# A two-layer graph network kernel: the opening chunks of x taken by rows, later ones by halves, and several steps in other places of the engines' orders

## What is computed

```python
def _ada_gcn(xn, weight, bias):                  # xn = x transposed: (N=512, B=64, L=128)
    x_norm = xn / jnp.maximum(jnp.linalg.norm(xn, axis=-1, keepdims=True), 1e-12)
    mean_sim = jnp.einsum('nbl,mbl->nm', x_norm, x_norm) / B
    k = max(int(N * 0.3), 1)
    ...                                          # keep the k most similar others of each node
    A = jnp.where(mask, mean_sim, 0)
    deg = A.sum(axis=0)
    dinv = jnp.where(deg > 0, jax.lax.rsqrt(deg), 0)
    An = dinv[:, None] * A * dinv[None, :]
    xw = jnp.einsum('nbl,lo->nbo', xn, weight)
    return jnp.einsum('sd,sbl->dbl', An, xw) + bias

x = _layernorm(x + L0(x, adj, bias))
x = _layernorm(x + L1(x, adj, W_lang, W_grav, W_V, W_O, gate_logit, log_sigma))
```

## Time and profile before

| | us |
|---|---|
| median of 3 runs | 957.14 (956.38 to 957.51) |
| the profiled execution | 958.09 |
| its span, first to last instruction | 956.4 |
| PE busy | 915.4 (96% of the span) |
| DVE busy | 750.3 (78%) |
| ACT busy | 535.0 (56%) |
| POOL busy | 306.9 (32%) |

### The profile page before, as it was taken

The page is one execution under the profiler, slowest core; times in us unless marked ns, Lnnn a source line. Parts: engine busy times, 40 slices in busy tenths (PEclk is TensorE's granted clock), DMA queues, the critical chain, the costliest instruction groups (busy, mean ns, idle before and its releaser), DMA issues.

```text
span 956.4 us, 18776 instructions
## 1 busy us (share of the span) xinstructions
PE 915.4 (96%) x6800; PEld 537.2 (56%) x6800; DVE 750.3 (78%) x1696; ACT 535.0 (56%) x956; POOL 306.9 (32%) x390
## 2 busy tenths in 40 slices
PE   3999999989999999999999999999999999999993
PEld 3777796555555555556464646555555555555451
DVE  5787398768888888888787888888887878786766
ACT  6787656675646455555546464646373646463531
POOL 3777372235040404040505050505050504041410
PEclk9999999999999999999999999999999999999997
DMA  6454230110413232313141413232222323121211
GB/s 266 176 200 155 87 90 1 45 45 6 96 57 88 64 81 66 89 53 104 38 119 29 116 33 109 42 101 48 94 55 87 58 84 71 73 57 45 56 46 44
DMA packets 101704, 75.84 MB, mean 79 GB/s; under 512 B 80544, under 2 KB 80672, under 8 KB 99616
## 3 DMA queue, kind: packets, MB, share of 16 engines
q1 hardware_dynamic: 101664, 75.32, 27.1%
HBM read 38.86 MB, written 16.78 MB: 58 GB/s over the span
## 4 chain that ended last, share of the span: by engine, by line
issue 50%; PE 19%; POOL 13%; DVE 11%; ACT 4%; DMA 1%; POOLq 1%; DVEq 0%; ACTq 0%
POOL arena L438 6%; PE bank L530 2%; PE bank L264 2%; PE bank L266 2%; PE bank L265 2%; POOL arena L443 2%; PE bank L537 2%; PE bank L536 2%; POOL arena L477 2%; ACT arena L1149 1%; POOL rn_parts L460 1%; POOL part_rest L458 1%; DVE stats L1636 1%; PE bank L500 1%; PE pair L264 1%
## 5 line engine op out<-in xcount | busy, mean ns | idle before, releaser
L264 PE MATMUL bank<-arena 128*128 128x512 f16 (+2 forms) x1056 | 293.8, 302 | 6.1 <-DVE arena L1690 2.0
L266 PE MATMUL bank<-arena 128*128 128x512 f16 (+2 forms) x1056 | 293.3, 301 | 0.0
L265 PE MATMUL bank<-arena 128*128 128x512 f16 (+2 forms) x1056 | 293.3, 301 | 0.0
L264 PE MATMUL pair<-arena 128*128 128x512 f16 (+1 forms) x400 | 151.2, 378 | 0.0
L265 PE MATMUL pair<-arena 128*128 128x512 f16 (+1 forms) x400 | 150.9, 378 | 0.0
L266 PE MATMUL pair<-arena 128*128 128x512 f16 (+1 forms) x400 | 150.8, 378 | 0.0
L264 PEld LDWEIGHTS bank<-arena 128*128 128x128 f16 x1056 | 103.6, 98 | 67.4 <-DVE arena L1690 4.3
L266 PEld LDWEIGHTS bank<-arena 128*128 128x128 f16 x1056 | 103.8, 98 | 63.5 <-issue 0.8
L265 PEld LDWEIGHTS bank<-arena 128*128 128x128 f16 x1056 | 103.8, 98 | 54.7 <-issue 0.3
L460 POOL TENSOR_TENSOR sq_parts<-cf,zero 128x4 bf16<-128x4 f32 x16 | 3.4, 210 | 397.2 <-DVE cf L1739 397.2
L438 POOL TENSOR_TENSOR arena<-arena 128x512 f32<-128x512 f32 x64 | 81.1, 1268 | 60.0 <-ACT arena L1059 59.6
(11 more groups left out here) (337 smaller groups left out, 1930.0 us busy)
## 6 DMA issues: line engine op xcount, KB each, us to landing
arena<-in_x SPq DMA_DIRECT2D x33, 1024.0 KB, 5.5
out_dram<-arena SPq DMA_DIRECT2D x15, 1024.0 KB, 4.3
arena<-arena SPq DMA_TRANSPOSE x75, 3.2
arena<-in_w_grav_t SPq DMA_DIRECT2D x1, 1024.0 KB, 7.4
arena<-in_w_lang_t SPq DMA_DIRECT2D x1, 1024.0 KB, 5.2
arena<-in_w_v SPq DMA_DIRECT2D x1, 1024.0 KB, 8.0
arena<-in_w_o_t SPq DMA_DIRECT2D x1, 1024.0 KB, 9.2
out_dram<-arena SPq DMA_DIRECT2D x4, 256.0 KB, 2.4
```

The source lines that it names most:

```text
L264: pe.matmul(dst, ah, bh, start=start, stop=False)
L265: pe.matmul(dst, ah, bl, start=False, stop=False)
L266: return pe.matmul(dst, al, bh, start=False, stop=stop)
```

## The change

It moves instructions and splits some. Of new work there are 29 small products on PE whose result nobody reads (`keep_warm`, into a bank that is cleared later), and three more waits per chunk in PE's loop. The parts:

1. Chunk 0 is loaded in two halves, and squared in one half and two rows. DVE adds its rows as they come.
2. ACT loads the table that has the root before its first instruction, and not ahead of the first root.
3. Chunks 0 and 1 are normalised and made high row by row; later chunks by halves. POOL makes low parts row by row for all chunks, and PE waits for each row.
4. `spread(c + 1)` stands ahead of the rows of chunk c, and no longer `spread(c + 2)`; `item_sums(c + 2)` in their middle, and no longer `item_sums(c + 3)`. ACT has a new order: second half of `high(c - 1)`, the squares of chunk c + 2, first half of `high(c)`, `root(c + 1)`.
5. `keep_warm(16)` before PE's first product, `keep_warm(9)` behind the first `item_sums`, `keep_warm(4)` behind the second.
6. POOL makes `mask` behind chunk 1 and not ahead of chunk 0.
7. The squares of W_V and adj stand behind ACT's copies of the turned blocks, in another buffer, and not ahead of `cross_out(0)`. `deviation(0)` stands ahead of the root of `magn`.
8. PE transposes `magn` behind chunk 2 of the second pass, and spreads the root behind chunk 4, not 1. DVE's maximum stands behind its first count, and `scales` behind its second.
9. On ACT `cross_out(2)` and `cross_out(3)` stand ahead of the high part of the first group's x.

PE at the program's start: before, the sums and spreads of three chunks stand ahead of the first row of products (L515 is the first product of a row).

The diff, cut to its core:

```diff
+            for half in range(2):
+                mine = slice(half * CL // 2, (half + 1) * CL // 2)
+                sp.dma_start(xc[0][:, mine, :], x_chunk[0][:, mine, :]).then_inc(s["first_half"] if half == 0 else x_loaded[0], 16)
-            for c in range(SLOTS):
+            for c in range(1, SLOTS):
                 sp.dma_start(xc[c], x_chunk[c]).then_inc(x_loaded[c], 16)
...
+            def keep_warm(n):
+                for i in range(n):
+                    pe.matmul(bank[4][:, 0:P], ones[:], ident[:], start=True, stop=True)
+
+            keep_warm(16)
...
+            def rows_01(c, slot, t, first=False, last=False):
+
+                pe.wait_ge(s["xn_l_ready"], c * CL + (t + 1))
+                gram(c, (0, 1), first=first, last=last, ts=range(t, t + 1))
 
             item_sums(0, 0)
+            keep_warm(9)
             spread(0, 0)
             item_sums(1, 1)
+            keep_warm(4)
+            rows_01(0, 0, 0, first=True)
+            rows_01(0, 0, 1)
             spread(1, 1)
             item_sums(2, 0)
-            rows_01(0, 0, first=True)
+            rows_01(0, 0, 2)
+            rows_01(0, 0, 3)
+            rows_01(1, 1, 0)
+            spread(2, 0)
+            rows_01(1, 1, 1)
+            item_sums(3, 1)
+            rows_01(1, 1, 2)
+            rows_01(1, 1, 3)
             with pe.Fori(0, (NC - 4) // 2) as j:
-                for t in (1, 2):
-                    rows_01(j * 2 + t, t % 2)
+                for u in (2, 3):
+                    c = j * 2 + u
+                    spread(c + 1, (u + 1) % 2)
+                    rows_01(c, u % 2, 0)
+                    rows_01(c, u % 2, 1)
+                    item_sums(c + 2, u % 2)
+                    rows_01(c, u % 2, 2)
+                    rows_01(c, u % 2, 3)
...
-                if c == 1:
+                if c == 2:
+                    pe.wait_ge(s["magn_ready"], 5)
+                    pe.wait_ge(s["magn_x"], 1)
+                    pe.transpose(bank[4][0:8, 0:P], magn[:], ident[:]).then_inc(s["magn_all_ready"], 1)
+                if c == 4:
 
                     pe.wait_ge(s["magn_root"], 2)
...
+            act.preload_act_table_set("sqrt_and_others")
...
+            def high(c, ts):
+
+                n = 1 if c < 2 else len(ts)
...
+            square(0, 0)
+            square(0, 1)
+            square(1, 0)
             root(0)
+            square(1, 1)
             repeat(0)
-            square(2)
-            for c in range(NC):
+            square(2, 0)
+            high(0, range(0, CL // 2))
+            square(2, 1)
+            root(1)
+            for c in range(1, NC):
+                repeat(c)
+                high(c - 1, range(CL // 2, CL))
+                if c + 2 < NC:
+                    square(c + 2, 0)
+                    square(c + 2, 1)
+                high(c, range(0, CL // 2))
                 if c + 1 < NC:
                     root(c + 1)
...
-            for n, i in enumerate((1, 0, 2, 3)):
+            for n, i in enumerate((1, 0, 3)):
...
+            act.wait_ge(s["w_in2"], 16)
+            act.activation(squares2, w_raw[2], ACT.Square, accum_out=magn[:, 2:3]).then_inc(s["magn_ready"], 1)
...
+            deviation(0)
             act.wait_ge(s["scale_steps"], 2)
...
+            cross_out(2)
+            cross_out(3)
             act.wait_ge(s["w_scaled"], 3)
             act.wait_ge(s["w_l_ready"], 2)
             act.activation(first_x_h, first_x, ACT.Copy).then_inc(s["x_h_ready"], GB)
 
-            cross_out(2)
-            cross_out(3)
...
             def normalise(c):
                 dve.wait_ge(s["spread_ps"], c + 1)
+                n = 1 if c < 2 else CL // 2
...
+                    between(i)
...
+            def scales(step):
+                if step == 0:
+                    dve.wait_ge(s["magn_all_ready"], 1)
...
+                if step != 1:
+                    return
```

More of the change, by code:

```diff
@@ L392, in _ @@
             pool.tensor_copy(ident_b[:], ident[:]).then_inc(s["picks_made"], 1)
[L393 to L407 removed]
+            for c in range(NC):
+                if c == 2:
+                    pool.wait_ge(s["small_in"], 64)
+                    pool.affine_select(out=mask[:], in_=adj_sb[:], compare_op=ALU.not_equal, fill=0.0, base=0,
+                                       pattern=[[-1, P]], channel_multiplier=1).then_inc(s["consts_made"], 1)
+                for t in range(CL):
+                    pool.wait_ge(s["xn_h_ready"], c * CL + t + 1)
+                    pool.tensor_tensor(xn_l[:, c * CL + t, :], xc[c % SLOTS][:, t, :], xn_h[:, c * CL + t, :],
+                                       ALU.subtract).then_inc(s["xn_l_ready"], 1)
             def low(dst, raw, hi, pieces, done):
@@ L551, in turn @@
                 return pe.transpose(dst, S[:, i, j * P:(j + 1) * P], ident[:])
-            def rows_01(c, slot, first=False, last=False):
-                if not isinstance(c, int) or c + 2 < NC:
-                    spread(c + 2, slot)
-                if first:
-                    for t in range(CL // 2):
-                        pe.wait_ge(s["first_low"], t + 1)
-                        gram(c, (0, 1), first=True, ts=range(t, t + 1))
-                else:
-                    pe.wait_ge(s["xn_l_ready"], c + 1)
-                    gram(c, (0, 1), ts=range(0, CL // 2))
-                if not isinstance(c, int) or c + 3 < NC:
-                    item_sums(c + 3, 1 - slot)
-                if first:
-                    pe.wait_ge(s["xn_l_ready"], 1)
-                gram(c, (0, 1), last=last, ts=range(CL // 2, CL))
+            def rows_01(c, slot, t, first=False, last=False):
+                pe.wait_ge(s["xn_l_ready"], c * CL + (t + 1))
+                gram(c, (0, 1), first=first, last=last, ts=range(t, t + 1))
@@ L582, in _ @@
+            for c in range(NC - 2, NC):
+                if c + 1 < NC:
+                    spread(c + 1, (c + 1) % 2)
+                for t in range(CL):
+                    rows_01(c, c % 2, t, last=(c == NC - 1))
             finish_diagonal(0)
@@ L943, in repeat @@
                                ACT.Copy).then_inc(s["rinv_ready"], 1)
-            def high(c):
-                act.wait_ge(s["xn_ready"], c + 1)
-                act.activation(xn_h[:, c * CL:(c + 1) * CL, :], xc[c % SLOTS], ACT.Copy).then_inc(s["xn_h_ready"], 1)
-            square(0)
-            square(1)
+            def high(c, ts):
+                n = 1 if c < 2 else len(ts)
+                for t in range(ts[0], ts[-1] + 1, n):
+                    act.wait_ge(s["xn_ready"], c * CL + t + n)
+                    act.activation(xn_h[:, c * CL + t:c * CL + t + n, :], xc[c % SLOTS][:, t:t + n, :],
+                                   ACT.Copy).then_inc(s["xn_h_ready"], n)
+            square(0, 0)
+            square(0, 1)
+            square(1, 0)
             root(0)
+            square(1, 1)
             repeat(0)
-            square(2)
-            for c in range(NC):
+            square(2, 0)
[9 more added lines that the diff above has]
+                high(c, range(0, CL // 2))
                 if c + 1 < NC:
                     root(c + 1)
-                    repeat(c + 1)
-                high(c)
-                if c + 3 < NC:
-                    square(c + 3)
+            high(NC - 1, range(CL // 2, CL))
             def s_out(dst, src):
@@ L978, in _ @@
                 act.activation(squares, w_raw[i], ACT.Square, accum_out=magn[:, i:i + 1]).then_inc(s["magn_ready"], 1)
-            act.wait_ge(s["magn_ready"], 4)
-            act.activation(squares[:, 0, 0:P], adj_sb[:], ACT.Square,
-                           accum_out=magn[:, 4:5]).then_inc(s["magn_ready"], 1)
             cross_out(0)
             cross_out(1)
-            act.wait_ge(s["magn_ready"], 5)
-            act.wait_ge(s["xn_l_ready"], NC)
+            act.wait_ge(s["magn_ready"], 3)
+            act.wait_ge(s["xn_l_ready"], NC * CL)
             act.wait_ge(s["gram_full"], 2)
@@ L1352, in _, with pick @@
             C, U = T + COUNTS, T + 2 * COUNTS
-            def pick(pair, n, between=lambda: None):
+            def pick(pair, n, between=lambda step: None):
                 r0 = 2 * pair
@@ L1394, in pick @@
                 n += 2
-                between()
                 for i in range(COUNTS):
```

86 lines of the change are left out of this document (46 added, 40 removed).

## The result

| | before | after |
|---|---|---|
| median of the runs | 957.71 us (20 runs, 956.24 to 959.95) | 953.67 us (20 runs, 951.43 to 956.53) |
| ratio | | 0.9956 [0.9948, 0.9964] |
| profiled execution, its span | 958.09, 956.4 us | 956.53, 954.8 us |

The change makes the kernel 4 us faster. The forecast was 5.2 us. The execution that was profiled here was the slowest of the 20, so the kernel after was profiled once more (experiment e12): 953.40 us, span 951.7.

A forecast was written before the change was run, and what follows sets the result against it. PE was taken to bound the kernel, idle mainly at the opening. The terms, -6.7 at the first pass's end and +1.5 in the second pass, make -5.2: 957.14 - 5.2 = 951.9 us, range 948.6 to 955.4.

The forecast's parts named there:

- The opening: Chunk 0 to the first pass's rows: first row of products at 15.7 against 23.7, rows done 8.4 us earlier on PE.
- Rival (c): First pass: the ring becomes the bound, PE waits at each spread, 0.6 us a chunk gives 959.1; chance 0.09.
- the ring: Each chunk's spread, normalise, high and low within one 5.38 us period; forecast to fit and priced at nothing.
- Rival (d): Opening: the warm-up does not raise the pace and delays the sums; 3.5 us lost, 955.4; chance 0.08.
- rival (a): PE's pace falls in a new idle time, at 12 to 15 or 101 to 104; costs 1.7 us, 953.6; chance 0.15.
- The end of the first pass: ACT, not PE, sets `cross_out(0)`: at 102.4, 6.7 us earlier, so 6.7 of PE's 8.4 us arrive.
- The second pass: Scales 3.8 us later, PE waits 1.2 at the turn and again before `first_project(0)`; PE 1.5 us late at the degrees.
- POOL's low part of x: Second pass: takes 6.07 us, ends at 146.6 in old times, and delays PE's `first_project(0)` by 0.8 us more.
- idle times of 1.2 us in the second part that cost nothing speak against: Argument against the pace falling in a new idle time: idle times of 1.2 us in the second part cost nothing.
- the stretch of the earlier trace: PE at granted clock 0.50 at 196 to 199, behind 2 us idle, costing up to 1.7 us; kept in the sum.

The follow-up runs named there:

- e12: The kernel after once more, unchanged, profiled again; 953.05 us, ratio 0.9956.
- e4: The kernel after without the three `keep_warm` calls of the opening; 954.92 us, ratio 0.9968.
- e7: The kernel after with 12 filler products and with part 9 alone undone; 955.46 us, ratio 0.9977.
- e1: The kernel after with parts 7 to 9 undone, so parts 1 to 6 alone; 956.86 us, ratio 0.9993.
- e9: Parts 1 to 6 and 9, filler products, e6's moved block product, squares of W_V and W_O on VectorE behind GpSimd's last low part; 949.50 us.
- e3: The kernel after plus 12 filler products nobody reads, 7 ahead of the first diagonal and 5 ahead of the turns; 953.79 us, ratio 0.9954.
- e6: e3 with a block column of the first group's upper product moved ahead of the turns of h for items 2 and 3; 951.48 us.
- e8: Parts 1 to 6 alone (e1) with the same 12 filler products as e3; 954.17 us, ratio 0.9970.
- e11: e10 with e6's moved block product in the first group; 953.79 us, ratio 0.9965.
- e10: Parts 1 to 6 and 9 with filler products (16 and 5), without parts 7 and 8; 954.97 us, ratio 0.9975.
- e5: e3 with the squares of two weights on VectorE in its idle time at 95.6 us and the scales at their old place; 956.33 us.
- e2: Parts 7 to 9 alone, on the kernel before; 958.50 us, ratio 1.0005.

## Why the prediction was right, and where it was not

**The opening: right.** `ssum(0)` was ready at 8.64 (forecast: 7.7). The second half of chunk 0 landed only at 6.5, which cost 0.9, and `keep_warm(16)` hid most of it, as it ended at 9.2 anyway. With the forecast in brackets, the sums started at 9.23 (8.9), the spread at 12.18 (11.9; but the terms that the prediction lists there, 9.8 + 0.7 + 1.05 + 0.63, make 12.2), the first row at 16.18 (15.7), and the spreads of chunks 3 and 4 at 27.83 and 33.27 (27.65, 33.05). From there a chunk took 5.38 us. Rival (c), the ring, did not occur. DVE and ACT grew by 0.13 and 0.12 us a chunk, under the 0.15 and 0.2 I had put on them, and POOL to 4.83 and not 4.51. Rival (d) is refuted by the rows at 16.46 and e4, and the fall of rival (a) in the opening did not occur in either profile of after; e7 shows that it can.

**The end of the first pass: right.** ACT and not PE sets it: `cross_out(0)` at 102.65 and 102.55 (102.4), 6.5 us earlier and not 8.4. e1 with one square more has 104.77, e9 with one less 101.01.

**The second pass: the mechanism right, one term too small.** With the clock held (e3) the scales' turn to wait came as written: ACT's high part of W_V at 114.55 (121.4 - 6.7 = 114.7), first group's x at 130.01 (129.4), the wait at the turn 1.08 us (1.2), the degrees at 160.73 (161.2). One step was wrong without harm: POOL's low part of x took 5.17 us and not 6.07, and PE did not wait for it; instead it waited 1.01 at the third diagonal, as ACT was still scaling x. The sum of the losses, 1.2 us, was forecast as 1.5.

What failed is the step "idle times of 1.2 us in the second part that cost nothing speak against" rival (a), and its price of 1.7 us. In the profiled execution of after the low stretch lasted from 104.3 to 111.1, not 3.5 us. From the first `turn` to the wait at the third diagonal PE needed 135.43 - 105.27 = 30.2 us, and 27.4 in e12 (105.16 to 132.56): **2.8 us for one fall of the clock**. The rival gave it a chance of 0.15 as something that happens or not; it happens in part of the executions. The 20 times of after go with the mean granted clock: five from 951.4 to 951.9 have 0.994, two of 956.5 have 0.987 and 0.989, and the rest lie between. Behind which gap each of them lost is not shown, but the profiles with 0.994 (e6, e8, e11) show no fall between 0 and 930 us.

**Two agreements are luck.** The five fast times lie at the forecast of 951.9, but the forecast had kept the stretch of the earlier trace rows in its sum. If they had no fall at all, what they saved there, 1.5 us in e12, made up for what the groups gave back. And the median, 953.7, is rival (a)'s 953.6 partly because before measured 957.71 beside it and not 957.14. As a distance the change is 4.0 us, between the forecast's 5.2 and rival (a)'s 3.5.

**A term that was missing: the groups.** I had taken what is gained at 166 us as gained at the end. Without a fall of the clock in the second pass that is 5.7 us (e3), and 4.2 arrive at the end. TensorE's waits at the same places of the groups, first before, then after:

```profile
206.51 0.22 PE L264 MATMUL bank<-adj_h,arena 128*128 128x128 f16 x1 [0.91 <-DVE arena L1690]
...
902.32 0.39 PE L264 MATMUL bank<-arena 128*128 128x512 f16 x1 [1.85 <-DMA arena<-arena]
```

```profile
204.17 0.22 PE L265 MATMUL bank<-adj_h,arena 128*128 128x128 f16 x1 [1.05 <-DVE arena L1746]
...
294.79 0.39 PE L265 MATMUL bank<-arena 128*128 128x512 f16 x1 [0.58 <-DMA arena<-arena]
...
311.04 0.23 PE L265 MATMUL bank<-arena 128*128 128x128 f16 x1 [0.44 <-DVE arena L1746]
...
901.59 0.39 PE L265 MATMUL bank<-arena 128*128 128x512 f16 x1 [1.81 <-DMA arena<-arena]
```

From the first to the last of each: 695.8 us before, 697.4 after. **1.6 us are given back in code that the change does not touch.** 1.04 of it falls in one group, with the wait of 0.58 for a transposed h to land and the one of 0.44 for DVE. The group before it is 0.2 longer, and from then on every second group is 0.09 longer (46.91 and 47.00 by turns, where before nearly all have 46.91). e1, e3, e6, e7, e8, e10, e11 and e12 show 697.1 to 697.7, e4 and e5 696.5 and 696.7, e2 696.2 and e9 696.0. So it comes with the new opening, in most of the kernels, and not with the clock, which is at 1.00 between these waits in all of them. Of the DMA queues after, 286 to 296 us (40 slices of 0.25 us: busy tenths, then GB/s; then the instruction queue):

```profile
DMA  2000000000089999599996899999000099899999
GB/s 45 0 0 0 0 0 0 0 0 0 6 184 219 209 202 183 120 222 213 210 206 125 187 214 273 196 112 25 2 8 9 10 306 336 287 377 393 377 377 377
...
q8 instruction: 1, 0.02, 0.7%
```

After the transposes the queues all but rest for 1.3 us (2 to 10 GB/s) at about 293, just when a piece of instructions is fetched, and the landing takes 4.5 us where the others take 3.3. The same coincidence stands in e3, e6 and e12, and in the profile of before no fetch falls into this place. In e9 a fetch does, the landings take 4.0 to 4.5 us too, and TensorE loses only 0.2. e10 has both cases: a fetch at 285, between two bursts, leaves the landings at 3.1 to 3.3, and one at 337, in the next group, stands beside landings of 4.5 and 5.1 and a wait of 0.58 at 340.27. That is still a coincidence, in seven traces. No run here moves the fetch alone, so the cause stays open, and so does what lengthens every second group.

At the very end the spans differ again: the last stretch, from the end of PE's last wait to the end of the span, is 15.4 us before (941.03 to 956.4), 14.5 after and 14.2 in e12, with the clock at 0.50 in a longer or a shorter part of it.

**The sum for the profiled execution**: 6.5 at `cross_out(0)`, less 1.2 for the second pass, less 2.8 for the clock, leaves 2.5 at the degrees; less 1.6 in the groups (and 0.1 ahead of them), plus 0.9 at the end, is 1.6 = 958.09 - 956.53 (1.56). For e12: 6.6 - 1.2 - 1.5 = 3.9; plus 1.5, because the stretch of the earlier trace rows ran at the full clock; less 1.9, plus 1.2: 4.7 (958.09 - 953.40).

## What to carry to other kernels

What an engine gains ahead of a joint arrives only as far as the slowest engine at the joint lets it, and the idle time that remains is not neutral: on TensorE it can cost the clock. Fill it with work, with real work first, and look at a second profile before you price it, since the clock may fall elsewhere instead. Price a move at the end of the program and not at the next joint: waits for DMAs and for VectorE in untouched code gave a quarter of it back here. VectorE's idle time beside a busy GpSimd is not free for instructions that read two operands from the same memory.

## What the runs showed of the hardware

**Whether the clock falls behind a gap differs from one execution to the next.** The same program with idle times of 1.58 and 1.15 us ran on at 1.2 GHz for 6.8 us in one execution, and at 2.4 GHz in another. The gap of 2.2 us at about 190 was followed by the low level in before, after, e2, e3, e7 and e10, and not in e1, e4, e5, e8 and e12; one of 3.00 (e7) and one of 4.16 (e1) were followed by it. With fillers at the end of the first pass seven profiles show no fall there (e3, e6 to e11), though 2.60 us of idle time are left in e8; e5 shows one, where waits of 1.77 and 1.95 us for GpSimd stood ahead of them. Without fillers after and e1 show one, e12 and e4 none. So the fillers make the fall rarer there, as far as so few profiles can tell, and e3, e7 and e10 have one at about 190 all the same. The Trainium skill ("TensorE: Matmul & The Clock Gate", section "What's actually happening") says that what watches the engine's activity runs free and is not reset by the kernel, so that the point of change moves between runs. The two executions of after agree with that.

**VectorE and GpSimd hold each other up.** Two squares of 128x2048 float32 with both operands in the arena (SBUF) took 3.22 and 2.86 us beside GpSimd (e5), 2.29 alone (e9), and GpSimd's four low parts 8.59 us for 4.51: 4.1 us lost on GpSimd for 6.1 us of VectorE's. The Trainium skill ("SBUF — State Buffer", section "SBUF: two separate sides") calls the port pair that the two share "an exclusive lock, not a bandwidth split", for VectorE instructions with two inputs in SBUF among others. The traces agree as far as they go: in e5 neither engine kept its own speed, in e9 both did.
